# A token tower on one core: the norm floor squared by ScalarE, the gate's epsilon folded into two products, the state product placed last, and new places for every step

## The reference, cut to what matters

```python
x = embed[tokens] + pos
for i in range(2):                          # the tower's layers
    h = ln(x)
    q, k, v = h @ wq + bq, (h @ wk + bk) / 4, h @ wv + bv        # 8 heads of 16
    k, v = causal_conv(filters, k), causal_conv(filters, v)
    Z = einsum('bhsd,bhse->bhsde', v, k)
    gates = relu(Z.reshape(.., 256) @ gate_k + gate_b) ** 2 + EPS
    attn = cumsum(gates * Z, 2) / (cumsum(gates, 2) + EPS)
    o = einsum('bhsd,bhsde->bhse', q, attn)
    o = o / max(norm(o, axis=3), EPS)
    x = x + o @ wo + bo
    x = x + gelu(ln(x) @ ff1 + b1) @ ff2 + b2
h = ln(x) @ out_k + out_b                   # width 256
h = h + linear_attention(layernorm(h))      # 16 heads of 64
h = h + (silu(g(n)) * u(n)) @ w_down        # n = layernorm(h), integer weights dequantized
```

## Time and profile before

| what | value |
|---|---|
| median of 3 runs | 1988.42 us (1988.13 to 1988.78) |
| the profiled execution | 1988.27 us |
| its span, first to last instruction | 1986.1 us |
| PE busy | 1850.2 us, 93% |
| DVE busy | 1165.6 us, 59% |
| ACT busy | 733.4 us, 37% |
| POOL busy | 439.4 us, 22% |
| mean granted clock of TensorE | 0.982 |

### The profile page before, as it was taken

How to read it: one execution, slowest core, us unless ns; L and a number is a source line. 1 busy time by engine, 2 the same in 40 slices (tenths; PEclk the granted TensorE clock), 3 DMA queues, 4 the chain that set the end, 5 groups by cost and what they waited for, 6 DMA issues and landing times.

```text
span 1986.1 us, 41766 instructions
## 1 busy us (share of the span) xinstructions
PE 1850.2 (93%) x17146; PEld 1588.0 (80%) x17146; DVE 1165.6 (59%) x3019; ACT 733.4 (37%) x1444; POOL 439.4 (22%) x391
## 2 busy tenths in 40 slices
PE   4799999999999999969899999999999999999998
PEld 3678888888888888758688888888888888888887
DVE  2668888888888888755554344434444444444443
ACT  1334444554455555334323322232233223322332
POOL 3233223333222222111121122112211221122112
PEclk8899999999999999989899999999999999999999
DMA  3000000000000000022000000000000000000000
GB/s 94 5 12 18 18 17 18 16 19 16 18 17 16 15 5 9 18 86 80 17 22 1 22 22 22 1 22 22 22 1 22 22 22 1 22 22 22 1 22 22
DMA packets 29211, 42.38 MB, mean 21 GB/s; under 512 B 5856, under 2 KB 22624, under 8 KB 29024
## 3 DMA queue, kind: packets, MB, share of 16 engines
q1 hardware_dynamic: 23648, 33.49, 5.1%
q0 software_dynamic: 2048, 4.20, 0.8%
q10 hardware_dynamic: 3328, 2.04, 0.4%
HBM read 22.93 MB, written 16.78 MB: 20 GB/s over the span
## 4 chain that ended last, share of the span: by engine, by line
PE 73%; DVE 17%; issue 4%; DMA 3%; POOL 2%; ACT 1%; SPq 1%; another core or an unknown queue 0%; DVEq 0%; POOLq 0%; ACTq 0%
PE ps L1406 11%; PE ps L1407 10%; PE ps L1408 10%; PE ps L806 3%; PE ps L1008 3%; PE ps L1456 3%; PE ps L1472 3%; DVE bxn L1271 3%; PE ps L887 3%; PE ps L807 3%; PE ps L808 3%; PE ps L959 3%; PE ps L937 2%; DVE bstats L1255 2%; DMA h<-h_rows 2%
## 5 line engine op out<-in xcount | busy, mean ns | idle before, releaser
L1245 POOL TENSOR_TENSOR hids_low<-hid,hids_high 128x512 fp32r<-128x512 f32 x96 | 137.6, 1440 | 611.0 <-ACT hids_high L1392 611.0
L512 POOL TENSOR_TENSOR rstd<-var,minus_half 128x4 f32<-128x4 f32 x80 | 82.5, 1032 | 564.5 <-DVE var L599 564.4
L757 ACT ACTIVATE xn<-x,shift,rstd 128x128 f32<-128x128 f32 x320 | 130.3, 482 | 133.6 <-DVE shift L604 133.6
L676 DVE TENSOR_TENSOR att<-ps,causal 128x512 f32<-128x512 f32 x256 | 158.6, 681 | 18.1 <-PE ps L937 18.0
L1406 PE MATMUL ps<-r_high,wq_high 128*128 128x256 f32 x512 | 147.4, 288 | 0.7 <-issue 0.7
L1407 PE MATMUL ps<-r_low,wq_high 128*128 128x256 f32 x512 | 144.9, 283 | 0.0
L1408 PE MATMUL ps<-r_high,wq_low 128*128 128x256 f32 x512 | 144.8, 283 | 0.0
L1386 ACT ACTIVATE silu<-ps 128x512 f32<-128x512 f32 x96 | 57.4, 598 | 226.5 <-DVE hid L1321 159.9
L1008 PE MATMUL ps<-w_f,wide 128*128 128x128 f32 x1024 | 130.1, 278 | 0.2 <-ACT wide L801 0.2
L1008 PEld LDWEIGHTS ps<-w_f,wide 128*128 128x128 f32 x1024 | 120.8, 192 | 6.0 <-issue 5.0
L1308 DVE TENSOR_TENSOR m_low<-ps,m_high 128x512 fp32r<-128x512 f32 x32 | 22.1, 692 | 170.8 <-ACT m_high L1378 170.8
(11 more groups left out here) (352 smaller groups left out, 5060.9 us busy)
## 6 DMA issues: line engine op xcount, KB each, us to landing
h_rows<-h_out SPq DMA_DIRECT2D x16, 512.0 KB, 2.8
h<-h_rows SPq DMA_DIRECT2D x16, 512.0 KB, 3.8
out<-bxn SPq DMA_DIRECT2D x32, 256.0 KB, 2.6
taps<-in_filters ACTq DMA_DIRECT2D x1, 1024.0 KB
emb<-in_embed,idx POOLq DMA_INDIRECT x64
wk<-in_W_kT SPq DMA_DIRECT2D x1, 1024.0 KB, 6.6
stage<-in_W_vT SPq DMA_DIRECT2D x2, 512.0 KB, 6.6
stage<-in_W_q SPq DMA_DIRECT2D x2, 512.0 KB, 5.6
```

Of the source, the lines that this page charges most:

```text
L512: pool.tensor_tensor(rstd[s][:], var[s][:], minus_half[:], ALU.pow)\
L676: dve.tensor_tensor(masked[:, :, PAIR * g:PAIR * g + PAIR, :], bank("qk", s, l, j, g, t)[:].rearrange("p (n r t) -> p n r t", n=2, r=PAIR) ...
L757: act.activation(xn[s][:, j, :], x[s][:, j, :], ACT.Identity, bias=shift[s][:, j:j + 1], scale=rstd[s][:, j:j + 1]).then_inc(xn_made[s].se ...
L1245: pool.tensor_tensor(hids[1][:, halves, :], hid[:, half, :], hids[0][:, halves, :].bitcast(F32), ALU.subtract).then_inc(hid_low[s].sem, 1)
```

## The change

Four edits to the tower and a new set of tables.

1. **Gate's epsilon.** The gates are kept without EPS. Bias and relu are one tensor_scalar, the square is a tensor_tensor, and EPS is added in the product with the keys, which is now two instructions (one for each head of a pair).
2. **Floor.** The running sums lack EPS once for each token. A small table `b_floor`, one number for each token, carries EPS times the count of tokens plus EPS. ACT reads the sums from PSUM and squares scale * sum + bias, in two instructions of 16 columns, as a step `floor` of its own. The bank of the state is free only after it. DVE's `state_low` keeps one instruction of three.
3. **State products last.** The state products leave `av` and become a step `apply` behind the four `av` steps, and add to what the bank holds.
4. **Places.** All of `PLACES_A`, `STARTS_A`, `PLACES_B`, `STARTS_B`, `PREPARE` and `START_UP` have new numbers.

```diff
-PLACES_A = [("embed", 0, 0, 750), ("stats", 0, 0, 601), ("pow", 0, 0, 868), ("shift", 0, 0, 710), ("xn", 0, 0, 874),
+PLACES_A = [("embed", 0, 0, 512), ("stats", 0, 0, 729), ("pow", 0, 0, 711), ("shift", 0, 0, 816), ("xn", 0, 0, 951),
...
-                   (b_gate[:], a["gate_b"].rearrange("l o -> o l").to_broadcast([P, L]))]
+                   (b_gate[:], a["gate_b"].rearrange("l o -> o l").to_broadcast([P, L])), (b_floor[:], a["b_floor"])]
...
-            dve.tensor_tensor(gate[s][:], gate[s][:], b_gate[:, l:l + 1].to_broadcast([P, J * HEADS]),
-                              ALU.add).then_inc(g.sem, 1)
+            dve.tensor_scalar(gate[s][:], gate[s][:], b_gate[:, l:l + 1], 0.0, ALU.add, ALU.max).then_inc(g.sem, 1)
             dve.wait_ge(g.sem, g.at(t, k + 3))
-            dve.scalar_tensor_tensor(out=gate[s][:], in0=gate[s][:], scalar=0.0, in1=gate[s][:],
-                                     op0=ALU.max, op1=ALU.mult).then_inc(g.sem, 1)
+            dve.tensor_tensor(gate[s][:], gate[s][:], gate[s][:], ALU.mult).then_inc(g.sem, 1)
             dve.wait_ge(g.sem, g.at(t, k + 4))
-            dve.tensor_scalar(gate[s][:], gate[s][:], EPS, None, ALU.add).then_inc(g.sem, 1)
-            dve.wait_ge(g.sem, g.at(t, k + 5))
             uses.wait_free(dve, ("gk", s, l, t))
-            dve.tensor_tensor(gk_heads[uses.place["gk", s, l, t]],
-                              kc[s][:].rearrange("p j (q r e) -> p (j q) r e", r=PAIR, e=HD),
-                              gate[s][:].rearrange("p (a r) -> p a r", r=PAIR).unsqueeze(3)
-                              .to_broadcast([P, J * PAIRS_A, PAIR, HD]), ALU.mult).then_inc(g.sem, 1)
+            for r in range(PAIR):
+                ins = dve.scalar_tensor_tensor(out=heads[:, :, r, :], scalar=EPS, in1=ungated[:, :, r, :],
+                                               in0=weights[:, :, r].unsqueeze(2).to_broadcast([P, J * PAIRS_A, HD]),
+                                               op0=ALU.add, op1=ALU.mult)
+            ins.then_inc(g.sem, 1)
...
-            dve.tensor_scalar(floor[s][:], bank("state", s, l, t)[:, NB * D:NB * D + J * HEADS], EPS,
-                              EPS_NORM, ALU.add, ALU.mult).then_inc(g.sem, 1)
-            dve.wait_ge(g.sem, g.at(t, 3 * l + 1))
-            dve.tensor_tensor(floor[s][:], floor[s][:], floor[s][:], ALU.mult).then_inc(g.sem, 1)
...
+        elif step == "floor":
...
+            act.wait_ge(state_step[s].sem, state_step[s].at(t, 2 * l + 1))
+            act.sem_inc(passed)
+            w = NB * HEADS
+            for c in range(C):
+                ins = act.activation(floor[s][:, w * c:w * c + w],
+                                     bank("state", s, l, t)[:, NB * D + w * c:NB * D + w * c + w], ACT.Square,
+                                     bias=b_floor[:, c:c + 1], scale=EPS_NORM)
+            ins.then_inc(state_step[s].sem, 1)
...
-            if j == NB:
-                pe.wait_ge(state_step[s].sem, state_step[s].at(t, 3 * l + 3))
...
-            if j >= NB:
-                b = j - NB
-                pe.matmul(out, state[s][:, b, :], qT_last[s][:, P * b:P * b + P], start=True, stop=False,
-                          skip_group_check=True)
...
+        elif step == "apply":
+            pe.wait_ge(state_step[s].sem, state_step[s].at(t, 2 * l + 1))
+            for b in range(NB):
+                ins = pe.matmul(bank("av", s, l, t)[:, P * (NB + b):P * (NB + b) + P], state[s][:, b, :],
+                                qT_last[s][:, P * b:P * b + P], start=False, stop=True, skip_group_check=True)
+            ins.then_inc(p_av[s].sem, 1)
```

More of the change, by code:

```diff
@@ L33 @@
 GK_SLOTS, ATT_SLOTS = 1, 2
-PLACES_A = [("embed", 0, 0, 750), ("stats", 0, 0, 601), ("pow", 0, 0, 868), ("shift", 0, 0, 710), ("xn", 0, 0, 874),
[L37 to L58, removed]
-            ("wo_out", 1, 0, 3303), ("stats", 3, 0, 3319), ("pow", 3, 0, 3600), ("shift", 3, 0, 3478),
-            ("xn", 3, 0, 3594), ("turn", 3, 0, 3494), ("high", 3, 0, 3617), ("low", 3, 0, 3511),
-            ("bias", 3, 0, 3787), ("f1", 1, 0, 3619), ("gelu", 1, 0, 3776), ("f1", 1, 1, 3620), ("gelu", 1, 1, 3806),
-            ("f1", 1, 2, 3637), ("gelu", 1, 2, 3822), ("f1", 1, 3, 3661), ("gelu", 1, 3, 3863), ("f2", 1, 0, 3653),
-            ("f2", 1, 1, 3683), ("f2", 1, 2, 3688), ("f2", 1, 3, 3777), ("f2_out", 1, 0, 3850),
-            ("stats", 4, 0, 3871), ("pow", 4, 0, 3882), ("shift", 4, 0, 3882), ("xn", 4, 0, 3986),
-            ("turn", 4, 0, 3921), ("high", 4, 0, 3996), ("low", 4, 0, 3977), ("head", 0, 0, 3977),
-            ("head_out", 0, 0, 3981), ("head", 0, 1, 3998), ("head_out", 0, 1, 3999), ("idx", 0, 0, 145),
-            ("gather", 0, 0, 1320), ("gather", 0, 1, 2415), ("gather", 0, 2, 2784), ("gather", 0, 3, 3374),
-            ("store", 0, 0, 3967)]
@@ L355, in token_tower @@
     gl_made = signals("gl_made", FC * L)
+    AV = J + 1
     p_xT = signals("p_xT", LN)
@@ L385, in claims @@
         elif step == "gate":
-            out.append(("tower", ("vg", s, l, t), gate_step[s], 6 * l + 1))
+            out.append(("tower", ("vg", s, l, t), gate_step[s], 5 * l + 1))
         elif step == "state":
-            out.append(("tower", ("state", s, l, t), state_step[s], 3 * l + 3))
+            out.append(("tower", ("state", s, l, t), state_step[s], 2 * l + 2))
         elif step == "qk":
@@ L406, in claims @@
         elif step == "gated":
-            out.append(("gk", ("gk", s, l, t), p_av[s], J * (l + 1)))
+            out.append(("gk", ("gk", s, l, t), p_av[s], AV * l + J))
         elif step == "mask":
-            out.append(("att", ("att", s, l, j, t), p_av[s], J * l + 2 * j + 2))
+            out.append(("att", ("att", s, l, j, t), p_av[s], AV * l + 2 * j + 2))
         return out
@@ L914, in tensor @@
                 pe.wait_ge(zeroed, 1)
-            out = claim(pe, "state", s, l, t, inputs=[(gate_step, 6 * l + 6)])
+            out = claim(pe, "state", s, l, t, inputs=[(gate_step, 5 * l + 5)])
             heads = gk_heads[uses.place["gk", s, l, t]]
```

151 lines of the change are left out of this document (92 added, 59 removed), and 6 rows, old and new, of the table PLACES_A.

## The result

The changed kernel takes 1903.9 us (median of 4 runs, 1901.9 to 1905.3) against 1988.6 us for the kernel before on the same chip: a ratio of 0.957, 95% interval 0.956 to 0.959. The profiled execution spans 1901.0 us, 85.1 us less than before.

What follows compares the result with a forecast made beforehand. PE was taken as the bound, with DVE close behind in the tower. Terms of 60 us off and 16 on took 1988.3 us to 1944 us, with a range from 1918 to 1973.

Steps and rivals of the forecast that it cites:

- waits that come back: Tower: PE would wait for DVE's masks in layer 1 and for f1's operand in layer 0, 12 us on.
- products last: Tower: state products behind the av blocks save 0.59 us in each of 32 visits, 19 us off, bounds 10 and 22.
- wait for the state: Tower: PE's wait for the state, 18.0 us in 27 waits, goes entirely.
- gate, layer 1: Tower, gk: the gate's shorter chain takes 3 us off; layer 1's new order puts 4 us on.
- the masks' wait in layer 1: Tower, layer 1: the second four masks come 0.6 us too late for av if state starts at gk.
- No sure gain: Layer 0's gk: first masks and wo_out now stand ahead of gate_mul; the gate's term was 3 us off, bounds 0 and 10.
- 4 us on: Layer 1's gk: masks ahead of gate_mul and one PE step less before state add 4 us, bounds 0 and 10.
- The rival of POOL holding up the gate: Tower: POOL blocks the new gate's two-operand DVE instructions, 16 or 32 us come back, 1968 us; chance 0.08.
- ACT's floors at nothing: Tower: two floor instructions of 16 columns on ACT cost 0 us, bounds 0 and 3.
- gram ... I take 14 us off: Attention stage: xns_low no longer runs beside POOL's hid_low, so gram's 15.7 us wait loses 14, bounds 0 and 16.
- keys and r: Attention stage: two narrow runs a group instead of four, 4 us off, bounds 0 and 7.
- hand-over: Between tower and attention stage: ACT's wait of 1.53 us for the first staged weights shrinks, 2 us off, bounds 0 and 4.

Runs made afterwards that it cites:

- undone_free: The changed kernel with the state products between the av blocks again, reading a constant matrix and so without the wait for the state's copy: 1921.6 us.
- apply_alone: The kernel before with one edit, the state products last, at the old places, with floor on DVE and the old gate: 1971.3 us, ratio 0.991.
- before_free: The kernel before with its state products reading a constant matrix, so that PE waits for no state copy: 1966.8 us.
- floor_undone: The changed kernel with both floor instructions on DVE again, ahead of the state's copy: 1912.8 us.
- embed_back: The changed kernel with POOL's embed of the next group behind pow of layer 3's norm again, not ahead of it: 1918.7 us.
- places_only: The code of the kernel before with the change's new tables, without the entries of floor and apply: 1969.8 us, ratio 0.989.
- code_only: The kernel before with the three code edits at the old places, floor on ACT behind the state's copy: 2047.0 us, slower by 2.9%.
- gram_clear: The changed kernel with POOL's rows_high ahead of the second hid_low, and POOL waiting for xns_low before that hid_low: 1891.0 us, 0.955 of the kernel before.

## Why the prediction was off

The sign and the list of places were right, and so were the ways in which the products and the state's wait gain. Three terms of the tower failed: the gate's (14.6 us off), the size of the state's wait (12.5) and the waits that come back (9.8). The prediction's terms for the tower are put on 26 of 32 visits, so that they stand beside the table of steps:

```
term                             predicted, 32   on 26   measured on 26
products last                              -19   -15.4   -14.3
wait for the state                         -18   -14.6   -27.1
waits that come back                       +12    +9.8     0
gate, layer 1                        -3 and +4    +0.8   -13.8
all else                                     0     0      -2.8
sum                                        -24   -19.4   -58.0
```

The first two rows split the 41.4 us of `av` and product: 14.3 is what undone_free shows for the place, and 27.1 is the rest.

- **"I take 0.54 ... 0.59 us in each of 32 visits"**: the sum is right, 0.55 (undone_free), but two errors of some 0.2 us cancel in it. The products' records run at 0.36 us, better than my best bound of 0.45. And between the blocks, without a wait, they cost 0.55 + 0.36 = 0.91 us and not 1.99 - 0.86 = 1.13, since the 1.99 of the earlier trace rows was read behind a wait.
- **"The 18.0 us go"**: they went, and the step that failed is the size. The 27.1 us hold two things that I had no term for: 6.0 us of the long visit near the start, and 3.4 at `av`'s first pair in layer 1, where PE waited behind ACT's `conv_out` and not for the state. What is left is the wait itself. The two runs without it show 0.80 and 0.81 us a visit, where the idle column has 0.69 and 0.65 over the same visits. I priced a wait by its idle entry, and from start to start it costs more. Why is only argued: the records behind a wait come slowly. The long visit is luck of the trace and no merit of the change.
- **"Two more DVE instructions of 0.67 us ... 0.2 us late ... I take 12"**: this is a step that failed in kind: nothing came back. The half of it in layer 0, `f1` waiting for `low`, is real where floor stands on DVE: apply_alone shows 7.2 us of it, while in before_free `low` holds up `head` instead (4.5 us). Another 5 us come back in both at `f2`, which I hadn't forecast, and the masks' wait in layer 1 shows in neither. The edit of floor, which I costed at nothing on ACT and at -18 with the state's wait, also takes 0.4 to 1.2 us of DVE work out from ahead of `low`. I had that in the diff and didn't subtract it from this chain. floor_undone puts it back and 8 us with it. And I let PE start `state` the moment gk was made; in the changed kernel gk is done 0.27 us (layer 0) and 0.58 us (layer 1, medians) ahead of it, which is about the 0.6 us of slack that layer 1 lacked.
- **"No sure gain"** and **"4 us on"** for gk: wrong by 14.6 us, the largest error. I saw in the earlier trace rows that the product took 1.16 us and wrote that collisions with POOL decide. I then looked at DVE's new order alone, and not at POOL's, where `embed` had moved from behind `pow` to ahead of it. embed_back puts it back and 14 us with it. The gate's own edit is worth nothing at PE: the `state` step takes 22.4 us with the old gate (places_only) and 22.3 with the new.
- **The rival of POOL holding up the gate** was the same mechanism with the wrong sign: I asked whether the new code could be hit, not whether the old one was and the new one would be spared.
- **ACT's floors at nothing**: no wait of PE that the new place causes is seen (277 ns each, 14.2 us busy for 64, since the two of a visit overlap), and code_only shows what cover is worth: at another place the kernel takes 108 us more (2047.0 against 1939.1), with `conv_out` and xn queued behind floor, and the granted clock lower.
- **"gram ... I take 14 us off"**: some 20 us were there to be had (44.5 against 32.0 us in ten groups in gram_clear), but the change got some 5. xns_low fell to 1.23 us as forecast, but gram takes 41.2 us for 44.5 in ten groups, some 5 us in 16, since the same hid_low now runs beside bxn, 2.35 instead of 1.38 us. I had written "bxn may meet a `hid_low`" and gave it nothing. gram_clear keeps it off both and gets 13.5 us more.
- **keys and r, hand-over**: keys and r lose 3.8 us in 10 groups, 6 in 16 (forecast 4); the hand-over 2.2 (forecast 2). The whole stage gave 16.4 us for 18, and that this fits is luck: gram gave a third of its term, and about 5 us come from steps that had none.

## What to carry to other kernels

Price an edit on every chain that its instruction stands on, not only on the one that it was made for: the floor's 0.8 us were in the way of the copy and, behind it, of `low`. Read a wait from start to start, over the whole step, before and after, and over the same visits: here the idle column had 80 to 86% of the state's wait, while gram's row of 9.9 and of 14.3 us went with steps that differ by 1.7 us in ten groups. Look for the one visit that differs from its kind before a sum is put down to the change. Where two engines collide, read the order of both: moving one POOL instruction by one position made and unmade 14 us, and moving a collision to another instruction of the same chain gains nothing until it lands beside work that nobody waits for.

## What the runs showed of the hardware

A collision with POOL isn't confined to instructions that read two operands from SBUF. These are DVE's instructions in the chain to bxn, in the changed kernel and in gram_clear (busy us, mean ns):

```profile
L1281 DVE TENSOR_SCALAR bxn<-h,bmv,brstd 128x256 f32<-128x256 f32 x128 | 73.7, 638 | 1.4 <-POOL brstd L1245 1.4
```
```profile
L1286 DVE TENSOR_SCALAR bxn<-h,bmv,brstd 128x256 f32<-128x256 f32 x128 | 59.0, 524 | 1.4 <-POOL brstd L1246 1.4
```

A tensor_scalar with one SBUF operand of 128x256 and two scalars for each partition takes 1.38 us for four alone and 2.35 beside POOL's tensor_tensor, and the small L647 above 0.80 beside embed, against 0.18 in layer 1. In the prediction I had weighed only the rule on two inputs. The same section of the Trainium skill (SBUF — State Buffer, Who interferes with whom) also lists tensor_scalar among the instructions that can take the port pair shared with GpSimd, and these rows agree with that.
